# The normalised x turned by DMA transposes in SyncE's queue, in place of TensorE transposes through PSUM

## The reference

```
x = x + attn_a(layernorm(x))   # 16 heads of 16; keys within 32 tokens or among the first 4; softmax
x = x + ffn(layernorm(x))      # gate and up 256 -> 768 from integer weights, silu(gate) * up, down
x = x + attn_b(layernorm(x))   # rotary q, k; exp(rotated scores) / sum(exp(unrotated scores)), causal
x = x + ffn(layernorm(x))
```

## Time and profile before

| | |
|---|---|
| median of 2 runs | 2088.84 us (2082.86 to 2094.81) |
| the profiled execution | 2086.18 us, its span 2084.1 us |
| PE, busy | 1814.1 us, 87% |
| ACT, busy | 1436.6 us, 69% |
| DVE, busy | 1423.0 us, 68% |
| POOL, busy | 789.0 us, 38% |
| mean granted clock of TensorE | 0.939 of full speed |
| DMA queue of SP | 128912 packets, 195.44 MB, 37.1% of 16 engines' span |

### The profile page before, as it was taken

One profiled execution on the slowest core, in us unless ns is written; L12 is line 12 of the kernel. 1 busy time (PEld: TensorE's weight loads), 2 busy tenths in 40 slices (PEclk: granted clock), 3 DMA queues, 4 the chain that ended last, 5 costly groups with the idle time before them and its releaser, 6 DMA issues.

```text
span 2084.1 us, 63373 instructions
## 1 busy us (share of the span) xinstructions
PE 1814.1 (87%) x25221; PEld 1137.5 (55%) x25221; DVE 1423.0 (68%) x2978; ACT 1436.6 (69%) x3591; POOL 789.0 (38%) x1140
## 2 busy tenths in 40 slices
PE   5577889999898999989899998989899998988785
PEld 3353556555564655556465555646555565655444
DVE  6373768677676867767686776768687676865634
ACT  2227777786867777686777768676776867677591
POOL 0513243433434343342434334243434424343431
PEclk7687999999999999999999999999999999998987
DMA  6223344243434424343442424343243435333321
GB/s 155 72 44 94 81 118 102 91 109 86 119 76 117 108 84 110 89 112 74 117 108 84 113 87 113 73 132 93 85 113 90 113 69 135 90 102 86 79 70 37
DMA packets 129204, 199.51 MB, mean 96 GB/s; under 512 B 26720, under 2 KB 60512, under 8 KB 128880
## 3 DMA queue, kind: packets, MB, share of 16 engines
q1 hardware_dynamic: 128912, 195.44, 37.1%
HBM read 67.87 MB, written 51.52 MB: 57 GB/s over the span
## 4 chain that ended last, share of the span: by engine, by line
PE 45%; ACT 20%; SPq 11%; DVE 9%; DMA 7%; issue 4%; POOL 3%; POOLq 0%; ACTq 0%; DVEq 0%
PE psum L1120 10%; SPq L634 8%; ACT psum L1236 8%; PE psum L1150 5%; ACT probs_B L1226 4%; PE psum L1138 4%; PE psum L1071 4%; PE psum L1017 4%; DMA pack_b<-src_b 4%; PE psum L1053 3%; SPq L667 3%; PE psum L1094 3%; ACT probs_A L1219 3%; PE psum L883 3%; PE psum L1084 3%
## 5 line engine op out<-in xcount | busy, mean ns | idle before, releaser
L1236 ACT ACTIVATE psum<-psum 128x512 f32<-128x512 f32 x1024 | 607.6, 604 | 118.0 <-PE psum L1017 116.5
L1659 POOL TENSOR_TENSOR h<-tmp,h 128x512 f16<-128x512 f32 x192 | 227.7, 1186 | 410.7 <-DVE h L1540 410.7
L1226 ACT ACTIVATE probs_B<-psum 128x512 f32<-128x512 f32 x640 | 333.3, 632 | 51.0 <-PE psum L1038 48.7
L1017 PE MATMUL psum<-pack_b 48*128 48x512 f16 x1024 | 181.7, 396 | 53.2 <-DMA pack_b<-src_b 31.9
L1120 PE MATMUL psum<-xT,w_g 128*128 128x256 f16 x1536 | 204.0, 276 | 13.4 <-ACT psum L1236 12.1
L1265 ACT ACTIVATE tmp<-psum 128x512 f32<-128x512 f32 x192 | 118.2, 616 | 138.4 <-PE psum L1120 125.7
L1676 POOL TENSOR_SCALAR_AFFINE_SELECT probs_B<-probs_B 128x256 f32<-128x256 f32 x512 | 194.0, 412 | 50.4 <-ACT probs_B L1226 50.4
L1236 ACT ACTIVATION_READ_ACCUMULATOR psum<-psum 128x1 f32 x1024 | 209.6, 205 | 0.0
L1120 PE MATMUL psum<-xT,w_u 128*128 128x256 f16 x1536 | 208.7, 276 | 0.0
L1138 PE MATMUL psum<-w_d,h 128*128 128x256 bf16 x1536 | 200.8, 274 | 8.3 <-POOL h L1659 7.1
L1523 DVE SCALAR_TENSOR_TENSOR tmp<-tmp,psum 128x512 f32<-128x512 f32 x192 | 130.2, 679 | 96.3 <-ACT tmp L1265 95.8
(11 more groups left out here) (150 smaller groups left out, 3210.5 us busy)
## 6 DMA issues: line engine op xcount, KB each, us to landing
pack_b<-src_b SPq DMA_DIRECT2D x768, 64.0 KB, 2.4
pack_a<-src_a SPq DMA_DIRECT2D x384, 64.0 KB, 2.3
x<-in_L_attn_a_x_dram SPq DMA_DIRECT2D x32, 512.0 KB, 4.2
o_scr_A<-o_raw SPq DMA_DIRECT2D x64, 256.0 KB, 2.5
o_scr_B<-o_raw SPq DMA_DIRECT2D x64, 256.0 KB, 2.4
xn<-o_scr_A SPq DMA_DIRECT2D x32, 256.0 KB
rden_on<-r_scr_A SPq DMA_DIRECT2D x32, 256.0 KB
x_scr<-x SPq DMA_DIRECT2D x16, 512.0 KB, 2.8
```

The lines of the kernel that those rows point to most:

```text
L1017: pe.matmul(score_bank("DP", n, q, e)[:, :], pack_b[r, j % 2, 0, 0, tile, t * P:(t + 1) * P], pack_b[r, j % 2, 0, 1, tile, :], start=True, ...
L1226: act.activation(probs["B"][:, i, :], score_bank("NP", n // 2, q, n % 2)[:, :], ACT.Exp, scale=SM_SCALE / W_SCALE ** 2)\
L1236: act.activation(bank[:, :], bank[:, :], ACT.Exp, scale=SM_SCALE / W_SCALE ** 2, accum_out=den[:, 0, j, 2 * tile + e, t:t + 1]).then_inc(d ...
L1659: pool.tensor_tensor(h[1][:, i % 2, :], tmp[:, i % 2, :], h[0][:, i % 2, :], ALU.subtract)\
```

## The change

The high and the low part are now formed in token order, from `xn`, in two new tiles `x_part` (128x4x256, f16): ACT copies all of `xn` in one instruction of 128x1024 (`XH`, `split_high`), DVE subtracts in one of 128x1024 (`X1`, `split_low`). Then SP turns each part with four DMA transposes, each from 128x256 of `x_part` to 128x2x128 of `xT`: step `X` for the high part, `X2` for the low. `X` also waits for the last product that read the same `xT`. PE's step `X` is gone, and PSUM's two banks with it. The readers wait for the transfers of a whole part (64 counts) where they waited for halves. The table `AT` has new numbers throughout, with the places of the new steps.

```
-USES = {"X": KT, "T": 1, "V": 1, "O": 1, "W": 1, "G": 1, "U": 1}
-TAKERS = {"X": "X1", "T": "T2", "V": "VC", "O": "OX", "W": "W1", "G": "H", "U": "I"}
+USES = {"T": 1, "V": 1, "O": 1, "W": 1, "G": 1, "U": 1}
+TAKERS = {"T": "T2", "V": "VC", "O": "OX", "W": "W1", "G": "H", "U": "I"}
...
-    "PBX": (1006.9,),
-    "PBXH": (1011.1,),
-    "PBX1": (1013.2,),
+    "PBXH": (1013.65,),
+    "PBX": (1007.46,),
+    "PBX1": (1016.12,),
+    "PBX2": (1014.68,),
...
+        x_part = [sb(f"x_part{i}", [P, NT, D], F16) for i in range(2)]
...
+            def turn_x(block, part, q):
+
+                ln = LN[NORM_OF[block], q]
+                sp.wait_ge((x_high, x_low)[part], ln + 1)
+                if part == 0 and X_READERS[block, q] is not None:
+                    sp.wait_ge(gu_ready, X_READERS[block, q] + 1)
+                for t in range(NT):
+                    sp.dma_start_transpose(XT_OF[block][part][:, :, t * P:(t + 1) * P], x_part[part][:, t, :])\
+                        .then_inc(xT_in[part], 16)
...
-            def turn_x(block, q):
-                banks = [gu("X", 0, block, q, k) for k in range(KT)]
-                for t in range(NT):
-                    pe.wait_ge(xn_ready, LN[NORM_OF[block], q] * NT + t + 1)
-                    for k in range(KT):
-                        last = pe.transpose(banks[k][:, t * P:(t + 1) * P], xn[:, t, k * P:(k + 1) * P], eye[:, :])
-                        if t == NT - 1:
-                            last.then_inc(gu_ready, 1)
-
             def x_there(block, part, k, q):
 
-                if part:
-                    pe.wait_ge(gu_taken, taken("X", 0, block, q, k))
-                else:
-                    pe.wait_ge(xT_high, LN[NORM_OF[block], q] * KT + k + 1)
+                if k == 0:
+                    pe.wait_ge(xT_in[part], (LN[NORM_OF[block], q] + 1) * 16 * NT)
...
-            def x_high(block, q):
-                for k in range(KT):
-                    act.wait_ge(gu_ready, made("X", 0, block, q, k))
-                    act.activation(XT_OF[block][0][:, k, :], bank_of("X", 0, block, q, k)[:, :], ACT.Copy).then_inc(xT_high, 1)
+            def split_high(block, q):
+                ln = LN[NORM_OF[block], q]
+                if ln:
+                    act.wait_ge(xT_in[0], ln * 16 * NT)
+                act.wait_ge(xn_ready, (ln + 1) * NT)
+                act.activation(x_part[0][:, :, :], xn[:, :, :], ACT.Copy).then_inc(x_high, 1)
...
-            def x_low(block, q):
-                given = XT_OF[block]
+            def split_low(block, q):
+                ln = LN[NORM_OF[block], q]
...
-                for k in range(KT):
-                    dve.wait_ge(xT_high, LN[NORM_OF[block], q] * KT + k + 1)
-                    dve.tensor_tensor(given[1][:, k, :], bank_of("X", 0, block, q, k)[:, :], given[0][:, k, :], ALU.subtract)\
-                        .then_inc(gu_taken, 1)
+                if ln:
+                    dve.wait_ge(xT_in[1], ln * 16 * NT)
+                dve.wait_ge(x_high, ln + 1)
+                dve.tensor_tensor(x_part[1][:, :, :], xn[:, :, :], x_part[0][:, :, :], ALU.subtract).then_inc(x_low, 1)
```

More of the change, by code:

```diff
@@ new lines @@
+    "W": (1032.23, 1032.25, 1054.15, 1057.66),
+    "W1": (1031.25, 1038.6, 1053.67, 1054.72),
+    "W2": (1042.34, 1047.35, 1061.75, 1074.38),
+    "PAT": (336.44, 338.89, 338.97, 341.78),
+    "PAT1": (334.29, 344.64, 345.73, 348.23),
+    "PAT2": (337.51, 347.47, 348.07, 351.88),
+    "PBT": (1019.48, 1019.49, 1022.57, 1024.69),
+    "PBT1": (1020.71, 1022.74, 1023, 1028.81),
+    "PBT2": (1026.92, 1028.9, 1029.34, 1034.35),
+    "OAOR": (793.71,),
+    "OAOL": (744.53, 746.45),
+    "OAOM": (788.61, 789.06),
@@ new lines @@
+    "OAOH": (789.64, 820.6),
+    "OAOW": (813.44, 824.47),
+    "OAO": (834.66, 841.71),
+    "OAOX": (839.68, 846.31),
+    "OBOR": (1450.86,),
+    "OBOL": (1449.84, 1480.03),
+    "OBOM": (1467.2, 1494.78),
+    "OBOH": (1468.47, 1497.4),
+    "OBOW": (1476.02, 1498.92),
+    "OBO": (1504.67, 1512.31),
+    "OBOX": (1516.13, 1518.59),
+    "F2L0": (1518.94,),
+    "F2L1": (1522.27,),
+    "F2L2": (1524.66,),
+    "F2L3": (1529.42,),
+    "F2L4": (1529.9,),
+    "F2L5": (1529.92,),
+    "F1L0": (856.41,),
@@ new lines @@
+    "F1L1": (858.81,),
+    "F1L2": (876.49,),
+    "F1L3": (877.9,),
+    "F1L4": (880.09,),
+    "F1L5": (881.1,),
+    "PBL0": (991.75,),
+    "PBL1": (997.3,),
+    "PBL2": (1003.15,),
+    "PBL3": (1008.03,),
+    "PBL4": (1008.67,),
+    "PBL5": (1008.78,),
+    "NAL0": (256.86,),
+    "NAL1": (264.9,),
+    "NAL2": (271.54,),
+    "NAL3": (281.72,),
+    "NAL4": (282.45,),
+    "NAL5": (288.37,),
+    "PAXH": (309.27,),
+    "PAX": (311.06,),
+    "PAX1": (309.97,),
+    "PAX2": (314.35,),
@@ new lines @@
+    "F2XH": (1531.49,),
+    "F2X": (1531.9,),
+    "F2X1": (1531.43,),
+    "F2X2": (1532.02,),
+    "F1XH": (883.74,),
+    "F1X": (860.89,),
+    "F1X1": (893.17,),
+    "F1X2": (875.67,),
+    "PBXH": (1013.65,),
+    "PBX": (1007.46,),
+    "PBX1": (1016.12,),
+    "PBX2": (1014.68,),
+    "F1G": (900.67, 921.03, 921.51, 941.18, 944.34, 963.12),
+    "F1GT": (900.34, 921.44, 923, 942.6, 942.69, 960.37),
+    "F1U": (906.5, 922.33, 940.01, 945.49, 960.31, 966.62),
+    "F1H": (903.77, 923.08, 925.9, 945.46, 952.75, 965.23),
@@ L226, in places @@
         puts("X", block, block + "X"), puts("XH", block, block + "XH"), puts("X1", block, block + "X1")
+        puts("X2", block, block + "X2")
     for block in FS:
@@ L348, in tile_jobs, with last_readers @@
     return found
+def last_readers():
+    found, held = {}, {}
+    for _, kind, _, block, q in STEPS:
+        if kind == "X":
+            tile = block == "F2"
+            found[block, q] = held.get(tile)
+            reads = (("G", block), ("U", block)) if block in FS else (("T", block), ("V", "V" + block[1]))
+            held[tile] = max(use for (k, _, b, r), use in GU.items() if r == q and (k, b) in reads)
+    return found
+X_READERS = last_readers()
 X1_JOBS = tile_jobs(("XA", "XL"))
@@ L528, in build @@
         xn_ready = sem("xn_ready")
-        xT_high = sem("xT_high")
+        x_high = sem("x_high")
+        x_low = sem("x_low")
+        xT_in = [sem(f"xT_in{i}") for i in range(2)]
         tanh_ready = sem("tanh_ready")
@@ L767, in _ @@
                     load_b(int(kind == "RL"), n, q)
+                elif kind in ("X", "X2"):
+                    turn_x(block, int(kind == "X2"), q)
                 elif kind == "XS":
@@ L1180, in program @@
                         o_step(block, n, q)
-                    elif kind == "X":
-                        turn_x(block, q)
                     elif kind == "G" and n == 0:
@@ L1319, in _ @@
                 elif kind == "XH":
-                    x_high(block, q)
+                    split_high(block, q)
                 elif kind == "GT":
@@ L1608, in _ @@
                 elif kind == "X1":
-                    x_low(block, q)
+                    split_low(block, q)
                 elif kind == "H":
```

122 lines of the change are left out of this document (31 added, 91 removed), and 74 rows, old and new, of the table AT.

## The result

The kernel of after takes **2719.09 us** (median of 2 runs, 2714.79 to 2723.38) against 2088.84: 630 us more, a ratio of 1.3055, 95% interval 1.2977 to 1.3134. The forecast was 2276 us within 2040 to 2750. The direction and the place were right, the size was not: 187 us forecast, 630 measured.

A forecast was written before the change was run, and what follows sets the result against it. TensorE was taken as the bound, busy 1814 of 2084 us. Stalls 28c - 6.65, clock +1.6, removed work -7.5 and vanished waits -6 gave 11.7 us a turn at c = 1.08: 2276 us, range 2040 to 2750.

The forecast's parts named there:

- The four formulas: TensorE's stalls a turn (one sequence's work): PB 0.7 + 7c, F2 0.9 + 7c, F1 7c - 4.25, PA 7c - 4.0 us.
- c: Time one DMA transpose takes in SyncE's queue: between 0.32 and 1.93 us, taken as 1.08.
- the two score pairs that were counted as 1.8 us of cover: At PB, TensorE's work between the normalised x and the projection, expected to hide 1.8 us of the chain.
- The page that gives 1309 ns a transpose: Skill page on one 128x128 block; if a rate, c is some 2.6 us and the forecast some 2950 us.
- I let 6 of them vanish: Of TensorE's 7.9 us a turn of waits not at the transposes, 6 were to disappear, bounds 3 and 7.9.
- the sum: All terms together: 28c - 18.55 us a turn, 11.7 us at c = 1.08, times 16 turns 187 us.
- the clock at 1.6 us a turn: Loss from TensorE's lower clock behind an added wait at F1 or PA: 1.6 us a turn, bounds 0 and 3.4.
- The removed work: TensorE's transposes of the normalised x and the wait ahead of them go: 7.5 us a turn saved.
- The break-even at c = 0.66: Transpose price in SyncE's queue at which the change neither gains nor loses time.
- the rival "faster": Transposes issue in SyncE's queue as cheaply as a plain store, c = 0.33: -7.3 us a turn, 1972 us; chance 0.15.
- The rival of the queue as the bound: SyncE's queue, with 41.9 us a turn to spare, decides from c = 1.31: 2379 to 2657 us; chance 0.26.
- falls by some 88 us: TensorE's busy time in the profile of after was to fall by some 88 us.

The follow-up runs named there:

- copies: The kernel of after with a plain copy of each 128x256 tile in place of its DMA transpose, so xT is not turned: 2410.07 us.
- old_order: The kernel of after, eight transposes a normalisation kept, with the table of places of the kernel of before: 2884.72 us.
- old_order_free: The kernel of after with the table of before and no transfers; the products read constants once x_part is ready: 2100.64 us.
- free_turn: The kernel of after, new table kept, without the transfers; the products read constants as soon as x_part is ready: 2187.61 us.
- fitted_fillers: The kernel of after with useless products ahead of TensorE's waits for both parts, numbers fitted by place (none ahead of F1's first): 2637.77 us.
- four_more: The kernel of after with four more transposes, of constants into an unread tile, behind each eight: 2857.99 us.
- order_alone: The kernel of before, TensorE still transposing, with the new table of after and step X set 3.5 places ahead of XH: 2240.29 us.
- one_per_part: The kernel of after with one 128x1024 DMA transpose for each part instead of four of 128x256, x_part laid out anew: 2287.35 us.

## Why the prediction was right in direction and wrong in size

- **The mechanism held, its parts less well.** TensorE waits at PB, F2, PA and F1 for the chain copy, issues, landing. The four formulas, with the run's median c of 1.25 us, give 9.5, 9.7, 4.8 and 4.5 us; the turn shown has 11.6, 7.0, 5.0 and 4.5, 28.1 us for 28.4. That the sum agrees so well is luck. The four chains are together 5.9 us longer than counted, because they start later and c is 1.28 to 1.38 in these groups, and the four covers are 6.2 us longer. At PB the two score pairs that were counted as 1.8 us of cover leave 0.28: x is normalised later against them than in before. And PB waits mostly for the high part, 7.5 us of 11.6, not for the low one as forecast.
- **The price of a transpose** was taken as 1.08 us and is 1.25 at the median, 1.33 over the run ((2721.7 - 882 - 1161) / 512). Between the two rows that bounded it the geometric mean was too low. Over the whole run, where single waits reach 15.8 us, the stalls are 31.3 us a turn instead of 23.6: 123 us of the 450 that were missed. The reason given for the higher price, elements placed one by one, does not show: the run has (174176 - 26720) / 512 = 288 packets under 512 bytes for each transpose, and copies has 272 for each plain copy of the same tile. The page that gives 1309 ns a transpose (the Trainium skill, VectorE: DVE Perf Modes, The three transpose paths) was near to one instruction's price, but it is no rate per 128x128 block: eight blocks took 1.30 us. What the prediction quoted of the other page, that transposing DMAs are as fast as regular ones (the Trainium skill, Advanced Engine Details and Errata, X-Bar Transpose), does not hold for the queue's time here: 1.25 against 0.62 us.
- **The step that failed first: "I let 6 of them vanish".** Other idle time is +5.9 us a turn instead of -6, 190 us of the miss. With the old table it is unchanged against before (216 us in old_order and in before). Against the same code without the transfers it is 21 us less (237 in old_order_free) and under the new table 24 us less (335 in free_turn), so the stalls of TensorE took at most 1.5 us a turn off its waits for others; the new table added 95 us. That the reordering of everything else has a price of its own was not in the sum at all.
- **The step that failed second: the clock at 1.6 us a turn.** It was worked out from one dip behind one 2 us wait. With eight waits a turn the stretch from 500 to 2400 has a mean of 0.82, and the same work takes 11.4 us a turn longer: 157 us of the miss in the book. fitted_fillers shows that some half of what the clock cost, 81 us at least, can be had back as time; the rest comes back as waits.
- **The removed work** was sized about right (142 us in the book for 120), but old_order_free shows that it was never worth that: 2101 us with a free transfer. The break-even at c = 0.66 and the rival "faster" rested on this. Under the old table there was no break-even above zero, and with plain copies under the new one, at 0.62 us each, the kernel takes 2410 us where the sum gives about 2070.
- **The rival of the queue as the bound** fell. Its own condition, c from 1.31, is met by the run's mean, and yet SyncE waits for 882 us. Its 41.9 us of spare time were counted in a turn of before; the stalls lengthen the turn and with it the spare time. four_more speaks against it: 320 us more of issuing cost 139 us.
- **The right sign for the busy time failed too:** "falls by some 88 us" became +95, by the clock.

What stays open: how much of order_alone's 149 us is the table and how much my place for `X`; and through which engine the other half of the clock's time is lost again. It is not tested either whether a table made for one_per_part would beat before; it ran under the two tables alone.

No version with the DMA turning that was run beats before. The best is one_per_part at 2287 us, 9.4% slower.

## What to carry to other kernels

Count DMA transposes by instruction, not by bytes: give one instruction the whole tile, and compare count times price plus landing with the work that the waiting engine has in between. Find out as well when the first of them can start: the copy ahead of it and what stands ahead of it in the queue put the start anywhere between 1.2 and 7.9 us behind the normalised x here. Do not let the waits of a bounding engine absorb a new stall in the sum unless a row shows two of them ending on the same thing; here at most 1.5 of 7.9 us a turn went. A change that comes with a new order of everything has two effects, and the order needs a run of its own on the old code, and the new code one on the old order.

## What the hardware showed that was not expected

- A DMA transpose has a nearly fixed price in the issuing queue: 1.25, 1.26 and 1.30 us for 64, 128 and 256 KB of f16, twice the 0.62 us of a plain copy. Its landing takes 2.4, 2.6 and 3.4 us, that of the copy 2.1.
- The transfers went from 129204 to 276661 packets, those under 512 bytes from 26720 to 174176, and the share of the DMA engines did not rise (37.1% and 35.0% of a span that is longer, 773 and 953 us of 16 engines' time). The small packets are no mark of the transposes: copies has 165984 of them. They hurt others little. Under the same table the landing of the packs (`pack_b`) is 2.5 us with all transposes in (old_order) and 2.4 in before, that of the 32 KB store `r_scr_A` 1.9 and 1.8, that of the 512 KB store `x_scr` 3.1 and 2.8. In after `r_scr_A` takes 3.9 us, but that belongs to the new table: it takes 3.8 in free_turn, which has no transposes.
- At a mean granted clock of 0.807, that is, with much time at the lower of the two levels of 1.2 and 2.4 GHz, TensorE needed 183 us more for the same products; 168 of them in the products that read the turned x. Useless products in its waits brought the clock to 0.903 and the time down by 81 us.
